# Attention and experts on one core: a listing paced at two scatters a step, an earlier first projection, and eight staging places for the last batch

## The reference, cut to what matters

```python
x = layernorm(x + attention(x))          # 16 heads of 16, rotary embedding, softmax over 1024 keys
# two groups g of 32 experts, top 2 of each, for all 8 * 1024 tokens
scores = softmax(x2 @ router_w);  weight, expert = top_k(scores, 2)
order = argsort(expert);  xs = x2[tok[order]]            # rows sorted by expert
y = ragged_dot(silu(ragged_dot(xs, wg)) * ragged_dot(xs, wu), wd)
out_g = zeros.at[tok].add(y * weight)
x = layernorm(x + (out_0 * 2 + out_1 * 2) / 4)
```

## Time and profile before

| what | us |
|---|---|
| median of 3 runs | 2739.4 (2738.84, 2739.4, 2759.41) |
| the profiled execution | 2749.05 |
| its span, first to last instruction | 2747.2 |
| TensorE busy in it | 2283.7 (83%) |
| VectorE, ScalarE, GpSimd busy | 1877.7, 1526.6, 1090.0 |

### The profile page before, as it was taken

How to read it: one execution, slowest core, us unless ns; L and a number is a source line. 1 busy time by engine, 2 the same in 40 slices (tenths; PEclk the granted TensorE clock), 3 DMA queues, 4 the chain that set the end, 5 groups by cost and what they waited for, 6 DMA issues and landing times. The chain is left out here.

```text
span 2747.2 us, 44206 instructions
## 1 busy us (share of the span) xinstructions
PE 2283.7 (83%) x12531; PEld 1149.5 (42%) x12531; DVE 1877.7 (68%) x3693; ACT 1526.6 (56%) x3206; POOL 1090.0 (40%) x963
## 2 busy tenths in 40 slices
PE   2999999999999999999999989983059998999900
PEld 1433333433433433433433333322037776777700
DVE  2988878888779778788778879512315544666766
ACT  0277777767676766766767757750013333333344
POOL 2221230343443444444335342325445554555543
PEclk7899999999999999999989989965579999999955
DMA  4423432533444444443543542223466645788782
GB/s 124 107 44 87 126 79 66 128 83 109 143 105 113 131 111 120 132 123 90 145 124 76 141 130 58 73 65 111 156 228 208 230 148 170 229 238 245 233 293 88
DMA packets 205593, 371.48 MB, mean 135 GB/s; under 512 B 31984, under 2 KB 145136, under 8 KB 201136
## 3 DMA queue, kind: packets, MB, share of 16 engines
q1 hardware_dynamic: 142864, 259.69, 34.7%
q0 software_dynamic: 27552, 75.40, 7.7%
q10 hardware_dynamic: 34944, 33.56, 4.1%
HBM read 206.62 MB, written 135.69 MB: 125 GB/s over the span
## 5 line engine op out<-in xcount | busy, mean ns | idle before, releaser
L939 DVE TENSOR_REDUCE maxima_sb<-ps_a 128x1 f32<-128x1024 f32 x1024 | 1227.1, 1219 | 311.8 <-PE ps_a L694 301.8
L570 ACT ACTIVATE probs_sb<-ps_b 128x512 f32<-128x512 f32 x2048 | 1093.6, 599 | 432.4 <-PE ps_b L684 425.3
L694 PE MATMUL ps_a<-k_stack_sb,q_stack_sb 48*128 48x512 f32 x2048 | 747.9, 457 | 110.9 <-DVE maxima_sb L939 66.6
L684 PE MATMUL ps_b<-q_stack_sb,k_stack_sb 50*128 50x512 f32 x2048 | 789.3, 466 | 12.7 <-issue 7.1
L694 PEld LDWEIGHTS ps_a<-k_stack_sb,q_stack_sb 48*128 48x128 f32 x2048 | 317.5, 192 | 712.3 <-DVE maxima_sb L939 379.6
L712 PE MATMUL ps_o<-probs_sb,v_sb_sb 128*32 128x512 f32 x4096 | 571.0, 631 | 12.7 <-ACT o_raw_sb L578 11.9
L1217 POOL DMA_INDIRECT y_dram<-y_rows_sb,spot_sb x318 | 304.9, 959 | 293.5 <-DVE y_rows_sb L1469 283.4
L684 PEld LDWEIGHTS ps_b<-q_stack_sb,k_stack_sb 50*128 50x128 f32 x2048 | 325.9, 190 | 111.2 <-ACT probs_sb L570 72.6
L1321 PE MATMUL ps_g<-w_gu_sb,x_cols_sb 128*128 x1272 | 357.5, 404 | 6.1 <-issue 2.9
L106 POOL DMA_INDIRECT rows_dram<-stage_sb,listed_sb x224 | 216.6, 967 | 335.9 <-PE ps_o L712 307.1
L1249 ACT ACTIVATE x_cols_sb<-ps_x 128x256 f32<-128x256 f32 x318 | 121.9, 383 | 255.9 <-issue 125.4
(11 more groups left out here) (158 smaller groups left out, 2071.2 us busy)
## 6 DMA issues: line engine op xcount, KB each, us to landing
x_rows_sb<-rows_dram SPq DMA_DIRECT2D x318, 128.5 KB
swapped_sb<-feat_qk_sb SPq DMA_DIRECT2D x64, 256.0 KB
parts_dram<-parts_q_sb SPq DMA_DIRECT2D x16, 1024.0 KB
parts_dram<-parts_k_sb SPq DMA_DIRECT2D x16, 1024.0 KB
q_stack_sb<-parts_dram SPq DMA_DIRECT2D x64, 256.0 KB
k_stack_sb<-parts_dram SPq DMA_DIRECT2D x64, 256.0 KB
w_gu_sb<-w_gu SPq DMA_DIRECT2D x8, 2048.0 KB, 20.2
back_sb<-y_dram ACTq DMA_DIRECT2D x64, 256.0 KB
```

The source lines that it names most:

```text
L570: act.activation(probs[t % NPR][:, j, :], src[:, :], ACT.Exp, scale=float(DH) ** -0.5).then_inc(s_bdrain, 1)
L684: pe.matmul(out[:, :], k_stack[u % NSTK][lo:lo + XROWS, jj, kc * P:(kc + 1) * P].bitcast(F32R), q_stack[u % NSTK][lo:lo + XROWS, jj, qh * ...
L694: ins = pe.matmul(out[:, kh, :], q_stack[u % NSTK][lo:lo + ROWS, jj, qt * P:(qt + 1) * P].bitcast(F32R), k_stack[u % NSTK][lo:lo + ROWS, j ...
L939: vec.tensor_reduce(maxima[u % 2][:, 1 - k, i:i + 1], src[:, :, :].rearrange("p a q -> p (a q)"), AX.X, ALU.max).then_inc(s_adrain, 1)
```

## The change

Three parts. The start: the projections of batch 0 wait for x_t, w_q, bias and w_k alone, which now raise `s_xt`; GpSimd's memset of the first value tile comes first; TensorE waits for the other constants only at the lead-in; the values and the second half (c = 1) of the first batch are projected before the lead-in, and that half's split is due at -28. The listing: due from step 31 on, two scatters a step, thus to step 46. The last batch: eight places in its first listing (four `back`, and eight `x_rows` as four pairs), all loaded ahead of the weights, one DMA for each choice's copy; the second listing keeps its four; `load_last` uses 24 semaphores and not one for each load.

```diff
-        for c, at in enumerate((start - 56, start - 24)):
+        for c, at in enumerate((start - 56, start - (36 if b == 0 else 24))):
...
-            put(b_jobs, start - 7 + i, "V", b, i)
+            put(b_jobs, start + i - (46 if b == 0 else 7), "V", b, i)
+LIST_AT, LIST_PACE = 31, 2
+        x_in = lambda b: 16 * (3 + b + 1)
-        k_step = lambda b, c: SPB * b + (-48, -16)[c]
+        k_step = lambda b, c: SPB * b - (48, 28 if b == 0 else 16)[c]
-                    pool_order.append((SPB * (b + 2) + 27 + 4 * t, "list", (b, t)))
+                    pool_order.append((SPB * (b + 2) + LIST_AT + LISTS // LIST_PACE * t, "list", (b, t)))
-            for dst, src in ((w_q, "w_q"), (bias, "bias"), (w_k, "w_k"), (consts, "consts"), (trig, "trig"), (w_v, "w_v"),
-                             (w_o, "w_o"), (bo_row, "bo_row"), (router, "router")):
+            for dst, src in ((w_q, "w_q"), (bias, "bias"), (w_k, "w_k")):
+                sp.dma_start(dst[:], dram[src][:]).then_inc(s_xt, 16)
+            for dst, src in ((trig, "trig"), (consts, "consts"), (w_v, "w_v"), (w_o, "w_o"), (bo_row, "bo_row"),
+                             (router, "router")):
                 sp.dma_start(dst[:], dram[src][:]).then_inc(s_par, 16)
-                        turns.append((SPB * (b + 2) + 27 + LISTS * (t - 1.5), 7, stage_in, (b, t)))
+                        turns.append((SPB * (b + 2) + LIST_AT + LISTS // LIST_PACE * (t - 1.5), 7, stage_in, (b, t)))
+            pool.memset(v_sb[0][:, :], 1.0).then_inc(s_ones, 1)
+            pool.wait_ge(s_ones, 1)
             for i in range(NSTK):
                 for n, lo in enumerate((SIDE // 2, SIDE + SIDE // 2)):
                     pool.memset(k_stack[i][lo:lo + SIDE // 2, :, :], -1.0).then_inc(s_ones, 1)
-            pool.wait_ge(s_ones, 2 * NSTK)
-            pool.memset(v_sb[0][:, :], 1.0).then_inc(s_ones, 1)
-                        pool.wait_ge(s_pv, min(SPB * (b + 2) + 26 + LISTS * t + n, n_steps))
+                        pool.wait_ge(s_pv, min(SPB * (b + 2) + LIST_AT - 1 + (LISTS * t + n) // LIST_PACE, n_steps))
-                if b == 0:
-                    pe.wait_ge(s_par, 16 * 9)
-                pe.wait_ge(s_xt, 16 * (b + 1))
+                pe.wait_ge(s_xt, x_in(b))
-            pe.wait_ge(s_ones, 2 * NSTK + 3)
-            pe.wait_ge(s_set, NSET)
             for t in range(first, steps_end):
+                if t == -LEAD:
+                    pe.wait_ge(s_ones, 2 * NSTK + 3)
+                    pe.wait_ge(s_set, NSET)
...
-    NSP = 2 * NY
+    NSP, NLS = 2 * NY, 24
+        def stage_of(m):
+            return (m, 1) if m < 2 * NBK else (m % NBK, m // NBK)
+        def stage_rows(m, kk):
+            slot, _ = stage_of(m)
+            return back[slot][:, kk, :] if slot < NBK else x_rows[TOPK * (slot - NBK) + kk][:, :]
         def load_stage(sp, m):
             n = (nb - 1) * KC + m % KC
-            if m >= NBK:
-                list_used(sp, m - NBK)
-            sp.dma_start(back[m % NBK][:, :, 0:D], dram["x1"][n * P:(n + 1) * P, :].unsqueeze(1).to_broadcast([P, TOPK, D])
-                         ).then_inc(s_stage[m % NBK], 16)
+            slot, _ = stage_of(m)
+            if m >= 2 * NBK:
+                list_used(sp, m - 2 * NBK if m < 3 * NBK else m - NBK)
+            for kk in range(TOPK):
+                sp.dma_start(stage_rows(m, kk)[:, 0:D], dram["x1"][n * P:(n + 1) * P, :]).then_inc(s_stage[slot], 16)
-                for m in range(KC - NBK, KC):
+                for m in range(KC) if g == 0 else range(KC - NBK, KC):
                     list_used(sp, g * KC + m)
+            if t >= NLS:
+                sp.wait_ge(s_last[t % NLS], 16 * (t // NLS))
-            for m in range(NBK):
+            for m in range(KC):
                 load_stage(sp, m)
             for c in range(W0_FIRST):
                 load_weights(sp, 0, c)
                 load_down(sp, 0, c)
-            for m in range(NBK, KC):
-                load_stage(sp, m)
...
+                slot, use = stage_of(m)
+                pool.wait_ge(s_stage[slot], 16 * TOPK * use)
                 for kk in range(TOPK):
-                    scatter_rows(pool, rows[:, kk, :], g, kk, keep["listed"][:, kk, g, at:at + 1], dram).then_inc(s_listed[m % NBK], 16)
+                    pool.tensor_copy(stage_rows(m, kk)[:, D:ROW].bitcast(I32), keep["place"][:, kk, n:n + 1]).then_inc(s_marked, 1)
+                pool.wait_ge(s_marked, TOPK * (m + 1))
+                for kk in range(TOPK):
+                    scatter_rows(pool, stage_rows(m, kk), g, kk, keep["listed"][:, kk, g, at:at + 1], dram).then_inc(s_listed[slot], 16)
```

More of the change, by code:

```diff
@@ L353, in stack @@
                     sp.wait_ge(s_bfill, b_no[("S", STEPS * (u - NSTK + 1) - 1, HEADS[-1])] + 1)
-                sp.wait_ge(s_ones, 2 * NSTK)
+                sp.wait_ge(s_ones, 2 * NSTK + 1)
                 for stk, which, runs in ((q_stack, 0, Q_RUNS), (k_stack, 1, K_RUNS)):
@@ L488, in _ @@
             pool.wait_ge(s_ones, 2 * NSTK + 4)
-            pool.wait_ge(s_par, 16 * 9)
+            pool.wait_ge(s_par, 16 * 6)
             for _, name, args in pool_order:
@@ L536, in features @@
                 if (b, c) == (0, 0):
-                    act.wait_ge(s_par, 16 * 9)
+                    act.wait_ge(s_xt, x_in(0))
                 elif q == 0:
@@ L546, in values @@
                     act.wait_ge(s_pv, SPB * (b - 1))
+                elif i == 0:
+                    act.wait_ge(s_ones, (1, 2 * NSTK + 2)[b])
                 act.activation(v_sb[b % 2][:, i * H * VW:(i + 1) * H * VW].rearrange("p (h d) -> p h d", d=VW)[:, :, 0:DH],
@@ L630, in values @@
                 out = b_tile()
+                if b == 0:
+                    pe.wait_ge(s_par, 16 * 6)
+                    pe.wait_ge(s_xt, x_in(0))
                 for dc in range(DC):
@@ L913, in between @@
                         room -= cost
-            vec.wait_ge(s_par, 16 * 9)
+            vec.wait_ge(s_par, 16 * 6)
             vec.memset(keep["count"][:, :, :], float(P)).then_inc(s_set, 1)
@@ L1106, in expert_phase @@
         s_back = [sem(f"back_in{i}") for i in range(NBK)]
-        s_stage, s_marked = [sem(f"stage_in{i}") for i in range(NBK)], sem("stage_marked")
-        s_listed = [sem(f"stage_listed{i}") for i in range(NBK)]
+        s_stage, s_marked = [sem(f"stage_in{i}") for i in range(2 * NBK)], sem("stage_marked")
+        s_listed = [sem(f"stage_listed{i}") for i in range(2 * NBK)]
         s_add = sem("row_added")
-        s_last = [sem(f"last_in{i}") for i in range(NB)]
+        s_last = [sem(f"last_in{i}") for i in range(NLS)]
         s_half, s_both = sem("second_choice_weighted"), sem("second_choice_added")
@@ L1175, in load_last @@
                          dram["y"][1][t * P * TOPK:(t + 1) * P * TOPK, :].rearrange("(p k) d -> p k d", k=TOPK)
-                         ).then_inc(s_last[t % NB], 16)
+                         ).then_inc(s_last[t % NLS], 16)
         @block.sync
         def _(sp):
-            for m in range(NBK):
+            for m in range(KC):
                 load_stage(sp, m)
@@ L1224, in list_stage @@
                 at = (nb - 1) % 2 * KC + t
-                rows = back[m % NBK]
-                pool.wait_ge(s_stage[m % NBK], 16 * (m // NBK + 1))
-                pool.tensor_copy(rows[:, :, D:ROW].bitcast(I32), keep["place"][:, :, n:n + 1]).then_inc(s_marked, 1)
-                pool.wait_ge(s_marked, m + 1)
+                slot, use = stage_of(m)
+                pool.wait_ge(s_stage[slot], 16 * TOPK * use)
                 for kk in range(TOPK):
-                    scatter_rows(pool, rows[:, kk, :], g, kk, keep["listed"][:, kk, g, at:at + 1], dram).then_inc(s_listed[m % NBK], 16)
+                    pool.tensor_copy(stage_rows(m, kk)[:, D:ROW].bitcast(I32), keep["place"][:, kk, n:n + 1]).then_inc(s_marked, 1)
+                pool.wait_ge(s_marked, TOPK * (m + 1))
+                for kk in range(TOPK):
+                    scatter_rows(pool, stage_rows(m, kk), g, kk, keep["listed"][:, kk, g, at:at + 1], dram).then_inc(s_listed[slot], 16)
             for m in range(KC):
@@ L1276, in weigh @@
             def weigh(t):
-                act.wait_ge(s_last[t % NB], 16 * (t // NB + 1))
+                act.wait_ge(s_last[t % NLS], 16 * (t // NLS + 1))
                 act.activation(last[t % NB][:, 1, :], last[t % NB][:, 1, :], ACT.Copy,
```

2 lines of the change are left out of this document (1 added, 1 removed).

## The result

| | before | after |
|---|---|---|
| median of 20 runs | 2759.88 us (2727.39 to 2784.85) | 2757.69 us (2742.79 to 2773.45) |
| profiled execution, its span | 2749.05, 2747.2 us | 2755.84, 2753.8 us |
| mean granted clock of TensorE | 0.907 | 0.893 |

The ratio after to before is 1.0055, 95% interval 1.0028 to 1.0081: 0.3 to 0.8% slower, inside the 1% that counts as no change. It leaves out runs more than 1.5% above a kernel's fastest, of which the kernel before had more; so the two medians lie closer together than the ratio. The forecast was 2696, 43 us off the median of three runs of the kernel before (2739.4); the twenty runs put that median 20 us higher.

What follows compares the result with a forecast made beforehand. TensorE sets the attention steps, and its stops also lower the granted clock. Start 6.4, listing 36.7 and last listing 5 made 48 us; 43 off the 2739.4 median gave 2696, range 2672 to 2730 (0.85).

Steps and rivals of the forecast that it cites:

- The start: Start and lead-in: TensorE starts 8.6 us earlier, lead-in gains 3.3 and loses 4 and 1.5; 6.4 us saved.
- Steps 62 to 64: End of batches 2 to 6: without late scatters behind the second split, these steps match batch 1; 30.8 us saved.
- steps 54 to 58: Batches 2 to 6: meetings of GpSimd and VectorE operations vanish, steps match batch 1's 18.7 us; 7.2 us saved.
- The rival that the stop at step 62 isn't the scatters': Batches 2 to 6, steps 62 to 64: the 30.8 us stays, time about 2722; chance 0.17.
- Two a step is 32 in 51.5 us: Listing at steps 31 to 46: pace of 0.62 scatters a us, near the free 0.565, costs 1 us a batch, 5 us.
- a rival, one or two stops of 6.2 us a batch at 0.16: Listing: two a step is itself a burst; one stop a batch 2723, chance 0.06; two or more 0.10.
- the rival's 2760: Listing: time if two a step costs two stops of 6.2 us a batch, 21 us slower; two or more stops 0.10.
- The order on SP: SP queue in attention: tile-2 staging load comes behind the k parts' store, ending TensorE's k_stack waits; 3.7 us saved.
- All staging turns come before the x1 store ...: nothing: Attention's end: the x1 store goes some 8 us later, but the block ends 30 us behind it; no cost.
- The last listing: Start of the experts: eight staging places bring the first row load 7 us earlier, less 2 us; 5 us saved.

Runs made afterwards that it cites:

- Experiment 9: Kernel of experiment 8, but in batches 2 to 6 each tile's four scatters go out together at the first of its four steps; ratio to the kernel before 0.9942.
- experiment 1: Kernel after, with the attention phase's listing back at one scatter a step from step 27; ratio to the kernel before 0.9952.
- Experiment 5: Kernel after, with four staging buffers and semaphores in the attention phase instead of two; ratio to the kernel before 0.9947.
- experiment 2: Kernel after, with staging loads that share the queue with the next stacks 1.5 steps later; ratio to the kernel before 1.0083.
- experiment 11: Kernel after, with four products a step that nobody reads in the last 26 steps of batch 7; ratio to the kernel before 0.9953.
- Experiment 3: Kernel after, with batch 7 listing at one scatter a step from step 27; ratio to the kernel before 0.9989.
- Experiment 6: Kernel after, with GpSimd held after tile 3 of the last unpaced listing until the router's last products; ratio to the kernel before 1.0058.
- experiment 8: Kernel after, with one scatter a step, tiles 0 to 3 at steps 31 to 46, 4 to 7 at 65 to 80, batch 7 as before; ratio 0.9833.

## Why the prediction was wrong

*The start (forecast 6.4, measured 6.6: 8.8 to the first exponential, less 2.2 in batch 0).* Right. First matmul 7.16 (near 7.5), last k_stack 49.42 (near 49.9). Up to the first exponential I had counted 10.4 and got 8.8: the lead-in's bare steps came 2.53 us apart as forecast, at a clock of 0.50, but the stage took 69.5 us, as long as before. Behind it the full steps at the low clock cost 2.2 us and not 4: one step took 3.91 us.

*Steps 62 to 64 (forecast 30.8, measured 30.8), steps 54 to 58 (7.2, measured 17.8).* The first is as forecast. For the second I took it that no meeting is left, and that is wrong in its mechanism. GpSimd and VectorE in step 55 of batch 3 (counted as in the earlier trace rows), after:
```profile
933.93 2.37 POOL L243 TENSOR_TENSOR feat_qk_sb<-feat_qk_sb,swapped_sb 128x1024 f32<-128x1024 f32 x1
```
```profile
935.26 1.07 DVE L786 TENSOR_SCALAR max_parts_sb<-maxima_sb 128x32 int32<-128x32 int32 x1
936.37 0.19 DVE L789 TENSOR_TENSOR max_parts_sb<-maxima_sb,max_parts_sb 128x32 f32<-128x32 f32 x1
```
VectorE's first piece ends with GpSimd's operation, at 936.3, and in each of the five batches it takes 1.1 to 1.8 us; before, it took 0.17 in batches 3 to 5. The second piece, 2.2 to 2.3 us long before in batches 2, 5 and 6, takes 0.19 in all. The rule of the Trainium skill (SBUF — State Buffer, on the engine ports) had one of the two engines hold the shared ports for its whole operation, so that an earlier split moves the meeting; the trace agrees. The split moved to a place where it costs less, and that it was not a dearer one was luck. Experiment 9 shows the other side: there such meetings went with 19 us more in steps 24 to 30. Another 6 us went in steps 1 to 30, which no term names. The rival that the stop at step 62 isn't the scatters' is dead: it went where the scatters went and came back with them in experiment 1.

*"Two a step is 32 in 51.5 us, 0.62, and not more, since a staging place is loaded again only when its scatters have landed. That is next to the free one. I take 1 us a batch."* This is the first of the steps that failed. It cost 7.7 us a batch in steps 31 to 46 (38.4 in five). The waits for staging, which I took for a brake, make the burst: with two buffers a load waits for the tile two before it, comes late, and the pace kept by step numbers then lets GpSimd catch up unchecked. Experiment 5 parts the 38, roughly: 23 for late loads, 15 for the pace. I had priced this as a rival, one or two stops of 6.2 us a batch at 0.16, and given its condition (GpSimd no longer waits between pairs). What stood in the earlier trace rows, a scatter at most each 2.6 us, and in the earlier trace rows, 0.565 a us, where the engines do other work, did not bear on pairs; the only dense row near these steps was the earlier trace rows, and it cost 6. That the measured time lies near the rival's 2760 is chance: these steps cost little more than one of its stops a batch, and the rest came from batch 7 and the exit.

*The order on SP (forecast -3.7, measured +9.5 of waits for k_stack apart from the start's).* "After, it comes behind" holds for the k parts (now at 622.54), but I didn't follow the queue one item on: the load of tile 2, at turn 32, stands ahead of the next batch's first stack, at 33, and blocks SP for tile 0's scatters. Yet experiment 2 shows that the waits are no cost of their own while GpSimd's burst is there.

*Batch 7 (in the forecast one of six equal batches; measured +31.1).* The second step that failed, a term that was missing. The forecast counted stops of TensorE with a low clock that comes back, as it does in the other batches. In batch 7 the maxima end at step 38, just behind the burst, and the clock stays low to the end. What is left is too little work: experiment 11 turned 117.8 into 81.4 us by adding some. Experiment 3 shows that removing the stop alone is not always enough, and the kernel before had lost the clock there too, but only for the last eight steps.

*"All staging turns come before the x1 store ...: nothing" (measured +8.0).* The third step that failed. The store is harmless, for from the last copy to the block nothing changed; what I missed is that the last listing now runs without a pause, and that its scatters hold VectorE and ScalarE: the router's stretch went from 21.7 to 29.7 us. Experiment 6 gave 7.4 us back.

*The last listing (forecast 5, measured 10.9).* The first row load came 6.1 us nearer, against 7. The last scatter started 24.6 us into the block, as forecast, and landed 7.88 us later, where it had taken 2.51: weights queued ahead of its count would explain that. The rule cited there (the Trainium skill, DMA: Bandwidth & Descriptors, on queues, rings and completion order) put the gain nearer 7 than 12, and this trace agrees. The rest of the block was 4.8 us shorter, which I can't place; in the other kernels with this part the block took 775.5 to 782.9 us, so 5 to 12 us are won.

So the terms for the start, for steps 54 to 64 and for the last listing came out as forecast or larger. The loss lies in three places in which scatters are dense, one of which costs through the clock.

## What to carry to other kernels

A pace kept by waiting for absolute step numbers is no pace once the engine is late: whatever delays it is followed by a burst, so count buffers and loads before raising the rate, or spread the work over more gaps at the old rate: here that took the ratio from 0.9952 (experiment 1) to 0.9833 (experiment 8). Cost a stop by what follows it in that stage: where the engine's work is thin afterwards, the clock doesn't come back. And when a queue item is moved, look at which item stands next behind it, in every batch.

## What the runs showed of the hardware

- Indexed scatters of 128 rows of 1028 bytes, sent by GpSimd back to back (one each 1.27 us), hold up the other engines' dependent instructions, up to 13.8 us at a time, on data that lie ready. Single ones at a step's distance (2.6 us or more) cost nothing in steps 31 to 46 (50.5 us with and without) and 1.2 us a batch in the second gap of experiment 8. Plain DMAs of the same size, one each 0.53 us, cost nothing in the router's stretch (10.6 us with them and without). The profile puts such waits down to "remote" or "issue". What inside an indexed scatter does it stays open: no run took the scatter apart.
- Adding products that nobody reads shortened a stretch from 117.8 to 81.4 us, by keeping the granted clock at 1.00 where it had been at 0.51.
